# A list-scheduled decoder kernel: when the planner takes a buffer as free again

## The reference

```python
x = x + local_attention(layernorm(x))          # 16 heads of 16, window of 7 tokens, q/k/v/o with bias
x = x + cross_attention(layernorm(x), ctx)     # 16 heads, 120 keys, q/k/v/o with bias
z = layernorm(x)                               # the last layer works on z
z = z + causal_attention(rmsnorm(z) * n1)      # 16 heads, causal mask, no bias
h = rmsnorm(z) * n2
z = z + (silu(h @ up.T) @ down.T) * top2_share(softmax(h @ gate.T))   # 1024 hidden features
x = x + z
```

## Time and profile before

| | |
|---|---|
| median of 3 runs | 4207.72 us (4207.07 to 4211.47) |
| the profiled execution's own time | 4207.72 us |
| its span, first to last instruction | 4206.0 us |
| PE busy | 3943.8 us, 94% |
| DVE busy | 2745.3 us, 65% |
| GpSimd busy | 2402.4 us, 57% |
| ACT busy | 1849.0 us, 44% |
| mean granted clock of PE | 0.987 of full speed |

### The profile page before, as it was taken

The page is one execution under the profiler, slowest core; times in us unless marked ns, Lnnn a source line. Parts: engine busy times, 40 slices in busy tenths (PEclk is TensorE's granted clock), DMA queues, the critical chain, the costliest instruction groups (busy, mean ns, idle before and its releaser), DMA issues.

```text
span 4206.0 us, 92442 instructions
## 1 busy us (share of the span) xinstructions
PE 3943.8 (94%) x38016; PEld 3128.5 (74%) x38016; DVE 2745.3 (65%) x5137; ACT 1849.0 (44%) x3393; POOL 2402.4 (57%) x2898
## 2 busy tenths in 40 slices
PE   4699999999999999999999999999999999999997
PEld 4477777777777777777777777777777777777776
DVE  4666666666666766766766766766766766766742
ACT  1344444444444444444444444444444444444442
POOL 4655655655655655655655655655655556556521
PEclk9799999999999999999999999999999999999999
DMA  4111111111111111111111111111111111111100
GB/s 146 47 42 64 39 57 64 39 57 62 36 61 53 43 64 45 51 64 43 53 64 41 55 64 41 56 64 39 58 64 39 58 64 39 57 64 39 57 7 8
DMA packets 87125, 221.25 MB, mean 53 GB/s; under 512 B 8316, under 2 KB 53688, under 8 KB 70328
## 3 DMA queue, kind: packets, MB, share of 16 engines
q1 hardware_dynamic: 86712, 215.34, 14.3%
HBM read 164.92 MB, written 50.39 MB: 51 GB/s over the span
## 4 chain that ended last, share of the span: by engine, by line
PE 54%; POOL 18%; DVE 14%; DMA 7%; issue 3%; ACT 2%; SPq 0%; POOLq 0%; DVEq 0%
POOL chunks L987 11%; PE ps L793 11%; PE ps L651 9%; DMA k_windows<-passed_k 7%; PE ps L700 6%; PE ps L635 5%; PE ps L731 5%; PE ps L784 5%; PE ps L670 4%; DVE nmax L1100 3%; PE ps L617 3%; POOL x L960 2%; PE ps L657 2%; DVE nmax_parts L1107 2%; POOL x L965 2%
## 5 line engine op out<-in xcount | busy, mean ns | idle before, releaser
L992 POOL TENSOR_TENSOR chunks<-v_windows,xT 128x560 f32<-128x560 f32 (+1 forms) x384 | 868.0, 2277 | 386.5 <-DVE xT L1077 264.8
L1100 DVE TENSOR_REDUCE nmax<-ps 128x16 f32<-128x1920 f32 (+2 forms) x320 | 714.7, 2234 | 419.7 <-PE ps L670 283.2
L987 POOL TENSOR_TENSOR chunks<-rest,k_windows 128x512 f32<-128x512 f32 (+1 forms) x384 | 554.8, 1453 | 691.9 <-DMA k_windows<-passed_k 684.6
L873 ACT ACTIVATE prob<-ps 120x1024 f32<-120x1024 f32 (+1 forms) x512 | 619.7, 1236 | 739.2 <-PE ps L708 738.6
L784 PE MATMUL ps<-xT,w_up 128*128 128x256 f32 x2048 | 505.7, 391 | 58.7 <-ACT xT L834 44.0
L1003 POOL TENSOR_SCALAR_AFFINE_SELECT prob<-prob 128x512 f32<-128x512 f32 x512 | 314.0, 639 | 386.1 <-ACT prob L873 386.1
L784 PEld LDWEIGHTS ps<-xT,w_up 128*128 128x128 f32 x2048 | 377.8, 192 | 145.2 <-ACT xT L834 57.0
L793 PE MATMUL ps<-w_down,held 128*128 128x256 f32 x2048 | 459.1, 382 | 2.2 <-DVE held L1145 2.2
L1057 DVE TENSOR_REDUCE xT<-chunks 128x32 f32<-128x512 f32 (+1 forms) x384 | 293.4, 764 | 253.9 <-POOL chunks L987 248.7
L1057 DVE TENSOR_REDUCE held<-chunks 128x80 f32<-128x560 f32 (+1 forms) x384 | 296.2, 771 | 242.7 <-POOL chunks L992 237.7
L793 PEld LDWEIGHTS ps<-w_down,held 128*128 128x128 f32 x2048 | 383.8, 190 | 62.2 <-issue 9.4
(11 more groups left out here) (139 smaller groups left out, 6889.6 us busy)
## 6 DMA issues: line engine op xcount, KB each, us to landing
k_windows<-passed_k SPq DMA_DIRECT2D x64, 1024.0 KB, 4.8
v_windows<-passed_v SPq DMA_DIRECT2D x64, 1024.0 KB, 6.9
x<-in_x SPq DMA_DIRECT2D x64, 256.0 KB, 3.0
passed_k<-rest SPq DMA_DIRECT2D x64, 256.0 KB, 2.0
passed_v<-held SPq DMA_DIRECT2D x64, 256.0 KB, 2.1
out<-x SPq DMA_DIRECT2D x64, 256.0 KB, 2.2
y<-in_ctx SPq DMA_DIRECT2D x64, 120.0 KB, 2.9
w_up<-in_up SPq DMA_DIRECT2D x1, 1024.0 KB
```

What stands on the lines that cost most here:

```text
L873: last = nc.scalar.activation(dst[0:keys], ps[0:keys, first:first + 4, n * T:n * T + dst.shape[2]], ACT.Exp, scale=SCALE)
L987: last = nc.gpsimd.tensor_tensor(chunk_of(c).rearrange("p (j d) -> p j d", d=D), q_row, window("k", (b + first) * D, (D, n), (1, D)), ALU. ...
L992: last = nc.gpsimd.tensor_tensor(chunk_of(c).rearrange("p (h i j) -> p h i j", i=HD, j=WINDOW), window("v", b * D + first * HD, (HD, n), ( ...
L1100: nc.vector.tensor_reduce(dst, src, AX_X, ALU.max, negate=True).then_inc(emptied[b], 1)
```

## The change

A part's places are given back in the event "free", at the planned end of the part, and no longer in the event "seen", a lag later. For the banks that is 0.15 us sooner in the plan (DVE or ACT drains them), for a `prob` buffer 0.21 us, for the windows 0.1 us, for the chunks 0.15 us, and for a lane 2.3 us: the lag of `store`. When parts become ready is computed as before. No instruction, size, place or semaphore is added or taken away; what can differ is the order of the parts on each engine and which place each gets.

```diff
@@ -263,9 +263,9 @@
             for what, n, i in events.pop(now):
                 if what == "free":
                     idle.add(parts[i].engine)
-                else:
                     for kind, use in parts[i].gives:
                         free[kind].append(self.slot[kind, n, use])
+                else:
                     for j in followers[i]:
                         missing[n, j] -= 1
                         if not missing[n, j]:
```

## The result

The changed kernel takes 4311.78 us (median of 4, 4310.35 to 4313.80) against 4209.50 us before (median of 4). The ratio is 1.0242, 95% interval 1.0222 to 1.0262: 102 us slower. The prediction was 4255 us, 47 us slower: the direction came out, and the size was less than half of what was measured.

The account below looks back on a forecast made before the run. PE's list was taken to bound the kernel, with DVE returning singles late. 4207.7 + 94 (turn's wait after the lane) - 47 (earlier head's gain), with 0 for banks and the rest, gave 4255 us, range 4155 to 4315.

Parts of the forecast that it names:

- What bounds the kernel: PE's list, busy 94% of the span; 2.34 us idle per period, 1.5 of it from singles DVE returns late.
- The lane: New sequence's head: load unmoved, turn planned 1.0 us too early, PE waits 1.6 us at 59 loads: +94 us.
- What the earlier head gives back: Window work moves ahead of DVE's saturated stretch, `up` banks return sooner: 0.8 us x 59 = -47 us, bounds 0 and -89.
- the shared port: DVE and GpSimd instructions shut each other out; collisions up to 2.3 us on round_max ahead of `shift`; no separate term.
- the emptied stretch: The 18.86 us per period with DVE busy 18.23, whose backlog shrinks, removing up to 1.5 us of PE waits.
- rival B: DVE's saturated stretch empties, PE's 1.5 us waits go, the turn waits only 0.2 to 0.6: 4165 us, chance 0.28.
- Banks, quad, prob, windows, chunks: Places free 0.1 to 0.21 us sooner in the plan, mattering only where PE decides inside that sliver: cost 0.
- The single spot that I followed: PE's wait at 2022.28: `up` goes before project_out but awaits the same ACT copy, wait stays 0.77 us, cost 0.
- Rival D: Pattern settles worse: a 2.3 us port collision on round_max delays `shift` and the next scores: 4330 us, chance 0.16.

Follow-up runs that it names:

- experiment 3: Changed kernel, same order, with ntop (minus the top logit) as a one-element tensor_reduce instead of tensor_scalar: 4186.78 us, ratio 0.9942 to the kernel before.
- experiment 9: Kernel before, order unchanged, with an extra unused DVE reduction of 2286 ns in the mean ahead of ntop: 4310.40 us, ratio 1.0242.
- experiment 2: Kernel before with everything but the lane given back at the planned end: 4276.03 us, ratio 1.0158 to the kernel before.
- experiment 8: Everything but the lane given back at the planned end, with ntop and both round_max casts as reductions: 4161.67 us, ratio 0.9875 to the kernel before.
- 6: Kernel before, old order, with ntop and both round_max casts as reductions: 4195.04 us, ratio 0.9966 to the kernel before.
- experiment 7: Only the lane given back at the planned end, with ntop and both round_max casts as reductions: 4238.00 us, ratio 1.0059 to the kernel before.
- experiments 4: Changed kernel with ntop and both round_max casts as one-element reductions, the subtraction between them unchanged: 4161.48 us, ratio 0.9880 to the kernel before.
- experiments 1: Kernel before with only the lane given back at the planned end, everything else when seen: 4464.86 us, ratio 1.0601 to the kernel before.

## Why the prediction was right in direction and wrong in size

That the kernel would be slower came out by luck. The forecast was a new wait of 94 us less a gain of 47; the new wait was a third of that, the gain was not to be seen in the time, and the loss came from a collision that the sum put at nothing. Without it the same order is faster than before (experiment 3).

*What bounds the kernel.* Right: PE's list does, and a delay of DVE in the stretch in which it is saturated came out at PE (101 of 146 us in experiment 9). One number there was loose: the order repeats, but SP's stores are 62.7 to 65.8 us apart, 63.4 in the mean of the first 59, so the window of 3583.60 us doesn't hold 57 periods exactly, and 2.34 us of idle per period is only about right.

*The lane.* The mechanism came as told: the load didn't move, the turn went ahead of the causal k projection, and PE got a new wait for ACT's norm. Its size was wrong: 1.6 us x 59 = 94 us were forecast; the row says 37.0 us in 68 waits, longest 5.1, most of them under 0.6 us, as the one with 0.29 us shown above. About 5 us of it were there before, so the new part is a third of the forecast. I read part of the difference as two things that were missed, which no run took apart. The down projection's drain no longer stood behind a window reduction, so the store came 8.1 us after the down projection's first matmul (2017.12 - 2009.00) instead of 9.1; and the chain from there to the turn took 8.9 us instead of the 9.4 estimated.

*What the earlier head gives back (-47 us).* This is the step that failed, and with it the 0 at which the shared port stood in the sum. The premise was that moving window work ahead can only unload DVE in the saturated stretch. It did remove the two waits of the earlier trace rows, but it also moved GpSimd's products, and one of them now covered ntop, ahead of two `up` drains. In place of a gain the waits for L1145 came, 46.9 + 42.6 + 12.1 us, and behind them the lower clock, 22 us on the down projection. Experiment 3 gives the price of that one instruction: 125 us. Without it, the sum "turn's wait minus the emptied stretch" is 4186.8 - 4210.6 = -24 us, which fits rival B's mechanism, priced at 4165: it seems to have been at work underneath. (Experiment 3 still has the waits of the turn and of round_max, so this is a net figure, not a proof.) I had priced the port only for round_max.

*Banks, quad, prob, windows, chunks (0).* Wrong for this kernel: alone they cost 65 us (experiment 2), and less than nothing once the three instructions can't be held (experiment 8 against 6). The single spot that I followed was read well: in experiment 2 `up` waits for the ACT copy in project_out's place, 45.2 us in 59 waits, 0.77 each. But there the swap of two parts also moved DVE against GpSimd, and I priced only PE's side of it.

*Rival D.* Right in mechanism and in the 2.3 us of a collision, wrong in the victim (round_max and `shift`) and given too low a chance (0.16). The evidence was in hand: collisions of 2.5 us at L1156, in 59 of its 64 instances and not in all 64 as the prediction has it, harmless, by the timeline, only by where they stood. My argument against it misread a row: L1107's median of 0.173 us doesn't say that most of round_max lies in the gaps, for 59 of its 128 instances take 1.47 us or more, and the mean shows it:

```profile
L1107 DVE CAST nmax_parts<-nmax 128x32 bf16<-128x32 f32 x128 | 100.3, 783 | 0.1
```

The Trainium skill, "SBUF — State Buffer", section "Who interferes with whom", lists copies, casts and tensor_scalar, and instructions with two SBUF inputs, as those that can contend with GpSimd for the shared ports (the latter with a GpSimd instruction that reads SBUF), and says that tensor_reduce never contends on trn2. The runs agree. A subtraction with two SBUF inputs (L1108) is held for up to 2490 ns, and ntop took 2075 ns in the mean as tensor_scalar, and 155 ns as tensor_reduce in the same order, with 154 to 158 ns over all 64. The copy of the logits out of PSUM, two instructions ahead of ntop, was never held either:

```profile
L1133 DVE COPY logits<-ps x64: 163/166/169, 239.7 to 4288.9; 128x16 f32<-128x16 f32 x64
```

Left open: how the 229 us that experiment 7 wins divide among its instructions and PE's clock, what the waits in the changed kernel would be without the clock's fall, and why the orders of experiments 4 and 8, so different, end within 0.2 us. The products and the subtraction with two SBUF inputs weren't rewritten in any run, nor was L1156 in the kernel before.

## What to carry to other kernels

In a kernel whose order is planned, a change of the planner can also change which small DVE instruction lies under a long GpSimd one, and that can be worth more (125 us here) than what the planner's change is about. The verdict turns with it: the changed order is 2.4% slower with the instructions as they were and 0.9% faster with three of them rewritten in both. So before judging an order, look in the table of instructions for tiny ones with means or maxima of microseconds, see which engine's instruction ends with them, and give them a form that isn't held; a free reduction over one element did it. And ask of each such wait not how long it is but who stands behind it: 2.5 us ahead of two drains cost 2.4% and more; behind the last drain they seem, by the timeline, to have cost next to nothing, which no run tested.

The fastest kernels found are experiments 4 and 8, 4161.5 and 4161.7 us, 1.2% below the kernel before. Which of the two orders is used makes no difference; both need the rewritten instructions.

## What the runs showed of the hardware

A DVE `tensor_scalar` of 128x2 took up to 2561 ns while GpSimd multiplied two SBUF tiles, and ended with GpSimd's instruction. When a held instruction was given another form, the next one in line that could be held was, in part: L1108 rose from a mean of 241 ns in experiment 3 to 646 ns in experiment 4. Where PE had waited 1.4 us for the v projection and 1.24 us for the down projection behind it, the granted clock fell to half in eleven of 30 sequences, and the down projections took 480.9 us in place of 459.1. I hadn't expected that taking the waits off three small instructions would be worth 6.0% - 0.6% = 5.4% in one order (experiments 1 and 7) and 0.3% in another (experiment 6).
